# The layers' norm with tokens on partitions

## The reference

```
for i in range(DEPTH):                      # DEPTH = 6
    x = attn_layer(shift_tokens(x), Wqkv[i], q_scale[i], k_scale[i], Wo[i]) + x
    x = ffn_layer(shift_tokens(x), ln_g[i], ln_b[i], W1[i], b1[i], W2[i], b2[i]) + x

def ffn_layer(x, g, bln, W1, b1, W2, b2):
    mu = x.mean(-1, keepdims=True)
    var = ((x - mu) ** 2).mean(-1, keepdims=True)
    xn = (x - mu) / jnp.sqrt(var + 1e-05) * g + bln
    hg = xn @ W1 + b1
    a, gate = jnp.split(hg, 2, -1)
    return a * jax.nn.gelu(gate, approximate=False) @ W2 + b2
```

## Time and profile before

| | |
|---|---|
| median of 3 runs | 3917.49 us |
| profiled execution | 3918.71 us, its span 3916.9 us |
| TensorE busy | 3581.4 us, 91% of the span |
| VectorE busy | 3162.1 us, 81% |
| ScalarE busy | 2652.5 us, 68% |
| GpSimd busy | 2432.0 us, 62% |
| mean granted TensorE clock | 0.98 |
| chain that ended last | PE 53%, DVE 15%, issue 9%, ACT 7% |
| products by `meanw` in the layers, L1236 and L1242 | 52.7 and 49.1 us busy, 96 records each for 48 groups |
| VectorE's passes of the norm, L955, L975, L978 | 678, 746, 1242 ns each, 48 of each |
| ScalarE's, L698, L703, L705 | 631, 682, 630 ns each, 48 of each |

### The profile page before, as it was taken

How to read it: one execution, slowest core, us unless ns; L and a number is a source line. 1 busy time by engine, 2 the same in 40 slices (tenths; PEclk the granted TensorE clock), 3 DMA queues, 4 the chain that set the end, 5 groups by cost and what they waited for, 6 DMA issues and landing times.

```text
span 3916.9 us, 146395 instructions
## 1 busy us (share of the span) xinstructions
PE 3581.4 (91%) x60128; PEld 2226.2 (57%) x60128; DVE 3162.1 (81%) x4377; ACT 2652.5 (68%) x4972; POOL 2432.0 (62%) x2197
## 2 busy tenths in 40 slices
PE   5676776899999999999999999999999999999997
PEld 2222222566666666666666666666666666666664
DVE  4899998888878778888878788778787887888884
ACT  3555554677777777767776777677777777676765
POOL 0355554876666666666666666666666666666661
PEclk9889898999999999999999999999999999999999
DMA  3000000111111111111110111111111111110101
GB/s 76 0 0 0 0 0 0 34 32 31 31 42 41 34 30 31 31 47 38 35 32 26 42 42 36 32 31 31 45 37 33 31 31 47 36 36 27 32 28 37
DMA packets 64418, 120.05 MB, mean 31 GB/s; under 512 B 18196, under 2 KB 35986, under 8 KB 63634
## 3 DMA queue, kind: packets, MB, share of 16 engines
q1 hardware_dynamic: 63762, 110.70, 9.7%
HBM read 20.50 MB, written 2.10 MB: 6 GB/s over the span
## 4 chain that ended last, share of the span: by engine, by line
PE 53%; DVE 15%; issue 9%; ACT 7%; POOL 0%; ACTq 0%; DMA 0%; DVEq 0%; POOLq 0%; SPq 0%
PE ob L1187 10%; PE qk L1129 9%; PE sc L1214 7%; PE trb L1001 6%; PE vob L1195 4%; PE vob L1135 4%; PE sc L1163 4%; DVE arena L888 3%; PE sc L1221 3%; DVE ssq L894 3%; DVE mx L901 3%; PE ob L1001 2%; DVE arena L889 2%; ACT arena L619 2%; DVE xnT L978 1%
## 5 line engine op out<-in xcount | busy, mean ns | idle before, releaser
L507 POOL TENSOR_TENSOR arena<-arena,rnorm 128x512 f32<-128x512 f32 x768 | 793.7, 1054 | 929.3 <-ACT rnorm L626 928.8
L500 POOL TENSOR_TENSOR arena<-arena 128x512 f32<-128x512 f32 x768 | 961.7, 1274 | 84.9 <-DVE arena L889 84.9
L633 ACT ACTIVATE arena<-trb 128x512 f32<-128x512 f32 x768 | 465.7, 606 | 432.4 <-PE trb L1001 432.4
L1129 PE MATMUL qk<-wqkv,xs 128*128 128x512 f32 x1536 | 734.2, 601 | 16.0 <-issue 8.9
L888 DVE TENSOR_TENSOR arena<-qk,tab_q 128x512 f32<-128x512 f32 x384 | 263.7, 687 | 504.6 <-ACT arena L619 499.6
L483 POOL TENSOR_TENSOR arena<-arena 128x512 f32<-128x512 f32 x256 | 299.9, 1180 | 345.4 <-DVE arena L858 329.9
L1001 PE MATMUL trb<-ident,arena 128*128 128x128 f32 x3072 | 483.0, 280 | 10.7 <-ACT arena L633 7.6
L619 ACT ACTIVATE arena<-qk 128x512 f32<-128x512 f32 x768 | 433.5, 592 | 79.4 <-PE qk L1129 65.5
L1129 PEld LDWEIGHTS qk<-wqkv,xs 128*128 128x128 f32 x1536 | 294.5, 193 | 312.0 <-issue 294.8
L894 DVE TENSOR_REDUCE ssq<-arena 128x16 f32<-128x1024 f32 x384 | 464.3, 1209 | 0.0
L514 POOL TENSOR_TENSOR arena<-arena,rinv 128x512 f32<-128x512 f32 x384 | 392.4, 1043 | 65.8 <-DVE rinv L911 65.8
(11 more groups left out here) (139 smaller groups left out, 6020.5 us busy)
## 6 DMA issues: line engine op xcount, KB each, us to landing
arena<-arena SPq DMA_DIRECT2D x192, 384.0 KB, 3.2
arena<-arena SPq DMA_DIRECT2D x192, 64.0 KB, 3.0
wqkv<-in_L_ffn_Wqkv SPq DMA_DIRECT2D x18, 512.0 KB, 4.3
wo<-in_L_ffn_Wo SPq DMA_DIRECT2D x6, 512.0 KB, 4.0
arena<-in_L_attn_x SPq DMA_DIRECT2D x8, 256.0 KB, 2.8
out<-arena SPq DMA_DIRECT2D x8, 256.0 KB, 2.2
w<-in_L_ffn_W SPq DMA_DIRECT2D x6, 341.0 KB, 2.9
arena<-in_sel SPq DMA_DIRECT2D x1, 1024.0 KB, 5.0
```

The lines of the kernel that those rows point to most:

```text
L500: nc.gpsimd.tensor_tensor(ts[c * 2 + j][:, heads], tu[:, 0, heads], tu[:, 1, heads], ALU.add).then_inc(summed[0], 1)
L507: nc.gpsimd.tensor_tensor(part, part, rnorm[j][:, 8 * h:8 * h + 8].unsqueeze(2).to_broadcast([P, 8, HEAD]), ALU.mult) \
L633: A((qT, kT)[j][u][:, 4 * h:4 * h + 4, at_col:at_col + P], TRB.rearrange("p (a t) -> p a t", a=4), ACT.Copy) \
L1129: MM(QK[:, 512 * h:512 * h + 512], lhsT=xs[u][:, c * P:(c + 1) * P], rhs=wqkv[:, col:col + 512], start=True, stop=True) \
```

## The change

The centred tokens, their squares and their sums are made with tokens on partitions. Per group: in slot 3 four turns bring `xs2` into `VOB` (now behind the `up` products), and VectorE's `centre` sums each token's 128 features along the free axis and subtracts the mean (now behind `hidden`); in slot 4 ScalarE squares and VectorE sums the squares, at the end of its slot; in slot 5 ScalarE takes Ln and Exp of 128x4 numbers, VectorE multiplies (behind `rope`), four turns, behind the down products, bring the result back into the second half of `SC`, and ScalarE copies it out to `xnT` with weight and bias. The odd `v_unit` waits for `centre` to have read `VOB`; `scores` of slot 6 waits for the copy out. The layer's parameters are copied in slot 5.

```diff
-LAG_STAGE, LAG_MEAN, LAG_VAR, LAG_NORMED = 17, 19, 21, 22
+LAG_STAGE, LAG_TOKENS, LAG_SQUARES, LAG_BACK = 17, 19, 20, 21
...
@@ ScalarE, layer_slot
                 unit = unit_at(l, k, 0)
                 if unit:
                     squares(*unit)
+                at_ = group_at(l, k, LAG_BACK)
+                if at_:
+                    act_e.wait_ge(n_var[0], at_[1] + 1)
+                    A(nlog[:], nvar[:], ACT.Ln, scale=1.0 / DIM, bias=eps[:, 0:1]).then_inc(n_log[0], 1)
+                    act_e.wait_ge(n_log[0], at_[1] + 1)
+                    A(nrstd[:], nlog[:], ACT.Exp, scale=-0.5).then_inc(n_rstd[0], 1)
...
-                at_ = group_at(l, k, LAG_MEAN)
-                if at_:
-                    item(act_e, ln_xc, at_[1] + 2 * GROUPS)
-                    A(sq2[0], xc[0], ACT.Square).then_inc(ln_sq[0], 1)
-                at_ = group_at(l, k, LAG_VAR)
-                if at_:
-                    item(act_e, ln_var, at_[1] + 2 * GROUPS)
-                    item(act_e, ln_out, at_[1] + (2 * GROUPS - 1))
-                    A(rstd[0], bank[2][:], ACT.Ln, bias=eps[:, 0:1]).then_inc(ln_log[0], 1)
-                    item(act_e, ln_log, at_[1] + 2 * GROUPS)
-                    A(rstd[0], rstd[0], ACT.Exp, scale=-0.5).then_inc(ln_rstd[0], 1)
+                at_ = group_at(l, k, LAG_SQUARES)
+                if at_:
+                    act_e.wait_ge(n_xc[0], at_[1] + 1)
+                    A(sq2[0], xc[0], ACT.Square).then_inc(n_sq[0], 1)
+                at_ = group_at(l, k, LAG_BACK)
+                if at_:
+                    if at_[0] == 0:
+                        item(act_e, lpar_done, l + (k - LAG_BACK) // LAYER)
+                    item(act_e, n_back, at_[1])
+                    A(xnT[:, at_[0] * GROUP:at_[0] * GROUP + GROUP], SC[:, 512:1024], ACT.Identity, scale=lpar[:, 0:1], bias=lpar[:, 1:2]) \
+                        .then_inc(n_out[0], 1)
...
@@ VectorE
+            def centre(group, n):
+
+                dve.wait_ge(n_turned[0], n + 1)
+                tokens = VOB[:, :].rearrange("p (c f) -> p c f", f=DIM)
+                V.tensor_reduce(nsum[:], tokens, op=ALU.add, axis=AX.X).then_inc(n_sum[0], 1)
+                slot(dve, n_back, n)
+                dve.wait_ge(n_sum[0], n + 1)
+                V.scalar_tensor_tensor(out=xc[0].rearrange("p (c f) -> p c f", f=DIM),
+                                       in0=nsum[:, :].unsqueeze(2).to_broadcast([P, GROUP // P, DIM]), scalar=-1.0 / DIM,
+                                       in1=tokens, op0=ALU.mult, op1=ALU.add).then_inc(n_xc[0], 1)
...
                 if unit:
                     rope(*unit)
+                at_ = group_at(l, k, LAG_BACK)
+                if at_:
+                    dve.wait_ge(n_rstd[0], at_[1] + 1)
+                    tokens = xc[0].rearrange("p (c f) -> p c f", f=DIM)
+                    V.tensor_tensor(tokens, tokens, nrstd[:, :].unsqueeze(2).to_broadcast([P, GROUP // P, DIM]), ALU.mult).then_inc(n_scaled[0], 1)
                 at_ = step_at(l, k, LAG_SCORES)
                 if at_:
                     maxima(*at_)
-                at_ = group_at(l, k, LAG_MEAN)
-                if at_:
-                    item(dve, ln_mean, at_[1] + 2 * GROUPS)
-                    V.tensor_tensor(xc[0], xs2.rearrange("p s t -> p (s t)"), bank[2][:], ALU.subtract).then_inc(ln_xc[0], 1)
...
                     hidden(*at_, 1, 4, 0)
                     hidden(*at_, 2, 5, 512)
+                at_ = group_at(l, k, LAG_TOKENS)
+                if at_:
+                    centre(*at_)
                 at_ = group_at(l, k, LAG_DOWN)
                 if at_:
                     add_y(*at_)
...
                 if unit:
                     square_sums(*unit)
-                at_ = group_at(l, k, LAG_NORMED)
...
-                    V.scalar_tensor_tensor(out=xc[0], in0=xc[0], scalar=lpar[:, 0:1], in1=rstd[0], op0=ALU.mult, op1=ALU.mult) \
-                        .then_inc(ln_aff[0], 1)
-                    item(dve, ln_aff, at_[1])
-                    V.tensor_scalar(xnT[:, at_[0] * GROUP:at_[0] * GROUP + GROUP], xc[0], lpar[:, 1:2], None, ALU.add).then_inc(ln_out[0], 1)
+                at_ = group_at(l, k, LAG_SQUARES)
+                if at_:
+                    dve.wait_ge(n_sq[0], at_[1] + 1)
+                    V.tensor_reduce(nvar[:], sq2[0].rearrange("p (c f) -> p c f", f=DIM), op=ALU.add, axis=AX.X).then_inc(n_var[0], 1)
...
@@ TensorE, layer_slot
-                mean = group_at(l, k, LAG_MEAN)
-                if mean:
...
-                    MM(VOB[:, :], lhsT=meanw[:], rhs=xs2.rearrange("p s t -> p (s t)"), start=True, stop=True).then_inc(ln_mean[0], 1)
-                var = group_at(l, k, LAG_VAR)
-                if var:
...
-                    MM(VOB[:, :], lhsT=meanw[:], rhs=sq2[0], start=True, stop=True).then_inc(ln_var[0], 1)
+                tokens, back = group_at(l, k, LAG_TOKENS), group_at(l, k, LAG_BACK)
...
                         up(*at_, parts, scored)
+                if tokens:
+                    pe.wait_ge(ln_in[0], tokens[1] + 1)
+                    if out_before:
+                        item(pe, x_added, out_before[0])
+                    for c in range(GROUP // P):
+                        last = turn(VOB[:, c * P:(c + 1) * P], xs2.rearrange("p s t -> p (s t)")[:, c * P:(c + 1) * P], start=True, stop=True)
+                    last.then_inc(n_turned[0], 1)
...
                     down_product(*at_, scored)
+                if back:
+                    pe.wait_ge(n_scaled[0], back[1] + 1)
...
+                    for c in range(GROUP // P):
+                        last = turn(SC[:, 512 + c * P:512 + (c + 1) * P], xc[0][:, c * P:(c + 1) * P], start=True, stop=True)
+                    last.then_inc(n_back[0], 1)
...
                 if value and k % 2:
-                    if mean:
-                        item(pe, ln_xc, mean[1] + 2 * GROUPS)
-                    elif var:
-                        item(pe, ln_log, var[1] + 2 * GROUPS)
+                    if tokens:
+                        pe.wait_ge(n_xc[0], tokens[1] + 1)
                     elif out_before:
                         item(pe, x_added, out_before[0])
                     v_unit(value[0], value[1], value[2], value[5])
```

More of the change, by code:

```diff
@@ L154, in build @@
         rnorm = [sb(f"rnorm{u}", [P, HEADS]) for u in range(2)]
+        nsum = sb("nsum", [P, GROUP // P])
+        nvar = sb("nvar", [P, GROUP // P])
+        nlog = sb("nlog", [P, GROUP // P])
+        nrstd = sb("nrstd", [P, GROUP // P])
         mx = [sb(f"mx{n}", [P, 2 * STEP_HEADS]) for n in range(2)]
@@ L314, in build @@
         x_added = sem("x_added")
+        n_turned = sem("n_turned")
+        n_sum = sem("n_sum")
+        n_xc = sem("n_xc")
+        n_sq = sem("n_sq")
+        n_var = sem("n_var")
+        n_log = sem("n_log")
+        n_rstd = sem("n_rstd")
+        n_scaled = sem("n_scaled")
+        n_back = sem("n_back", 1)
+        n_out = sem("n_out")
         up_done = sem("up_done")
@@ L965, in layer_slot @@
                     add_y(*at_)
+                at_ = group_at(l, k, LAG_BACK)
+                if at_ and at_[0] == 0:
+                    layer = l + (k - LAG_BACK) // LAYER
+                    if group_at(l, k, LAG_DOWN):
+                        item(dve, x_next, layer * GROUPS + -1)
+                    V.tensor_copy(lpar[:], lpar_all[:, ds(layer, 1), :].rearrange("p o n -> p (o n)")).then_inc(lpar_done[0], 1)
+                    item(dve, lpar_done, layer)
                 if unit:
                     square_sums(*unit)
-                at_ = group_at(l, k, LAG_NORMED)
+                at_ = group_at(l, k, LAG_SQUARES)
                 if at_:
[L970 to L974, removed]
-                    V.scalar_tensor_tensor(out=xc[0], in0=xc[0], scalar=lpar[:, 0:1], in1=rstd[0], op0=ALU.mult, op1=ALU.mult) \
-                        .then_inc(ln_aff[0], 1)
-                    item(dve, ln_aff, at_[1])
-                    V.tensor_scalar(xnT[:, at_[0] * GROUP:at_[0] * GROUP + GROUP], xc[0], lpar[:, 1:2], None, ALU.add).then_inc(ln_out[0], 1)
+                    dve.wait_ge(n_sq[0], at_[1] + 1)
+                    V.tensor_reduce(nvar[:], sq2[0].rearrange("p (c f) -> p c f", f=DIM), op=ALU.add, axis=AX.X).then_inc(n_var[0], 1)
             dve.wait_ge(lpar_in[0], N_LPAR)
@@ L1141, in windows, with scores @@
                         yield b, g, g // 2 * P + b * SPAN + g % 2 * WINDOW
-            def scores(s, B, u, j, n, up0, up1, up2, down):
+            def scores(s, B, u, j, n, up0, up1, up2, down, back):
                 item(pe, tr_evac, B * (2 * UNITS) + (2 * UNITS - 2 + j))
@@ L1155, in scores @@
                     item(pe, x_next, down[1])
+                if back:
+                    pe.wait_ge(n_out[0], back[1] + 1)
                 for h in range(2):
@@ L1198, in up @@
             def up(group, n, parts, scored):
-                pe.wait_ge(ln_out[0], n + (1 + 2 * GROUPS + ln_out[1]))
```

(19 more changed lines are left out.)

9 lines of the change are left out of this document (1 added, 8 removed).

## The result

The changed kernel takes 4103.69 us, the median of four runs (4093.57 to 4106.04); the kernel before 3916.15 beside it (four runs). The ratio is 1.047, 95% interval 1.0447 to 1.0493. The forecast was 4078 us, the range 3975 to 4155: slower, as forecast, by 187 us instead of 161. The profiled execution took 4093.57 us, 175 more than that of before, with a granted clock of 0.952 in the mean (before 0.980).

A forecast was written before the change was run, and what follows sets the result against it. TensorE was taken to bound the layers. The profiled 3918.7 us plus 99 for stalls (2.16 per group, 46 groups) plus 61 for the clock minus 1.2 gave 4078 us, range 3975 to 4155.

The forecast's parts named there:

- The wait in slot 3: Slot 3: TensorE's odd value product waits 2.86 us for VectorE's centring; slot takes 10.78 us, +1.11 per group.
- The old wait: Slot 3: the mean product's wait for VectorE's add into xT, 57.7 us in 46 times, would be covered.
- slot 7: Slot 7: the up products lose their wait for the normed rows, -0.43 us per group.
- Slot 5: Slot 5: the turn back waits 1.24 us for VectorE's scaling, +0.93, plus +0.55 for GpSimd's interference, per group.
- the half clock: Slot 4, at 1.2 GHz: a late unit product delays ScalarE and VectorE alike, so the fall isn't made good.
- the collision with GpSimd: Slot 5: VectorE's scaling multiply meets GpSimd's two-input instructions, +0.55 us; ends 0 and 1.04.
- the lower end of my term: Slot 5: the scaling multiply finds a gap between GpSimd's instructions and loses 0 us.
- The upper end: Slot 5: a whole GpSimd instruction is ahead of the scaling multiply, costing 1.04 us.
- The clock: After slot 3's gap TensorE's clock halves in 3 of 4 groups, 1.78 us each: 1.34 per group, 61 us.
- gaps of 1.1 us amid the small products of `values`: Earlier trace: two gaps of some 1.1 us there were read as leaving TensorE's clock alone.
- the upper bound of the term: Slot 3: TensorE's clock falls behind the new gap in every group, 82 us.
- Rival 3: Slot 3's odd value product: VectorE isn't late, TensorE runs through; 119 us faster, 3799 us; chance 0.06.

The follow-up runs named there:

- b_norm21: The kernel before, with the norm's last two passes (weight, bias) at the end of VectorE's slot 5 instead of slot 6; 0.9925 of before.
- a_fill: The changed kernel with three useless 128x512 products in front of TensorE's wait for the centred tokens in slot 3; 1.0353 of before.
- a_centre: The changed kernel with VectorE's centring in front of the two hidden steps in slot 3 instead of behind them; 1.0381 of before.
- a_fs: The changed kernel with the scaling ahead of the rotation in slot 5 and three useless products before slot 3's wait; 1.0047 of before.
- c_tok2: The changed kernel with centring ahead of the rotation in slot 3, scaling right behind the add into xT in slot 5; 0.9832 of before.
- b_all: The kernel before with the mean product behind the up products, its subtraction before slot 3's rotation, the norm's last two passes in slot 5; 0.9819 of before.
- a_scale: The changed kernel with VectorE's scaling ahead of slot 5's rotation and ScalarE's small Ln and Exp ahead of its squares; 1.0206 of before.
- c_tok: The changed kernel with the scaling ahead of the rotation in slot 5 and the centring ahead of the rotation in slot 3; 0.9898 of before.

## Why the prediction was right

**The wait in slot 3** was the main term and came out as worked out. In the three periods in which the clock didn't fall in it the slot takes 10.75 us; the prediction said 10.78. The sum (0.68) and the subtraction (0.69, taken as 0.74) were priced from neighbours within 0.05.

**The old wait** is gone from slot 3 and the one of **slot 7** too (7.32 in the ordinary slots), as predicted; b_norm21 shows the latter alone.

**Slot 5** was put at +0.93 +0.55; its middle value is +0.73 (9.76), its mean +1.04 (two periods, in which the clock fell in slot 5, take 13.7 and 14.1). Two errors. The scaling started 4.38 us into the slot, not 4.70: I had said that the half clock delays VectorE and TensorE alike in slot 4, so that nothing is made good; in fact VectorE came out of it some 0.3 to 0.4 earlier relative to TensorE (the clamp L915 that ends slot 4's sums of squares is over at 2152.49, 0.40 before slot 5 starts; in the earlier trace rows it is over 0.01 after). Where the clock had not fallen, it started at 4.71, as worked out. And the collision with GpSimd cost 0.26 in the middle (0.94 instead of 0.68), not 0.55. It hangs on a few hundredths of a microsecond. In a_fill the multiply starts at 4.71, 0.03 ahead of GpSimd's next instruction, and takes 0.68: the lower end of my term, 0.

```profile
2145.97 0.68 DVE L983 TENSOR_TENSOR arena<-arena,nrstd 128x512 f32<-128x512 f32 x1
2146.00 3.02 POOL L513 TENSOR_TENSOR arena<-arena 128x512 f32<-128x512 f32 x2
```

The upper end, 1.04, was met too: with it the multiply takes 1.72, and it took 1.71 in a_centre, started 0.10 behind GpSimd's, and 1.60 to 1.81 in five groups of the changed kernel. The Trainium skill says (SBUF — State Buffer, "Who interferes with whom") that a VectorE instruction with two SBUF inputs and a GpSimd instruction that reads SBUF exclude each other, and that the order of issue decides who waits. These rows agree.

**The clock** was mis-sized. I took falls in 3 of 4 groups at 1.78 us, 1.34 per group. It fell in slot 3 in 41 of 44 and in slot 4 in one more, and a period with falls costs 0.9 in slot 3 and 1.1 in slot 4 over the clean values (11.65 and 9.16 in the middle, against 10.75 and 8.05). Slots 3 and 4 together are +3.02 us per group where my terms made 2.45: 26 us over 46 groups. Slot 5, 0.44 below its terms, took back 20 of them. With the 8 us outside the 46 periods the profiled execution is 14 us over the sum (175 against 161), and the other three took 8 to 12 us more than it, which makes the 26 by which the forecast is short of the median. That the fall itself costs, and not only the wait, is what a_fill and a_fs show.

One reading behind the 3 of 4 was wrong: that gaps of 1.1 us amid the small products of `values` left the clock alone. The trace of before has three of 1.12, each at the end of a layer, and behind two of them the clock fell (at 2229.20 and at 3297.71). Here is the first, with the window behind it:

```profile
2229.20 0.42 PE L1187 MATMUL ob<-arena 64*64 64x32 f32 x11 [1.12 <-issue]
...
2230.04 1.86 PE L1135 MATMUL vob<-wqkv,xs 128*128 128x512 f32 x2
2231.70 2.78 PE L1129 MATMUL qk<-wqkv,xs 128*128 128x512 f32 x4
```

```profile
2230.20:2233.40 3.20, 3.20 (x5) 1.13 (x4) 0.61 (x3) 2.47 (x5) 0.00 (x0) 0.50 0.02 5
```

These rows speak for a higher share of falls than 3 in 4 behind the longer gap of slot 3, toward the upper bound of the term.

What the prediction's sum has no term for are the gaps amid small products in slots 3 to 5: 23 in slot 3 of the changed kernel, of some 0.76 us. They cost nothing there, since TensorE then waits for `centre` anyway; in the faster kernels they are what is late next.

Rival 3, the gain from TensorE's shorter program, was real potential. Something like the 0.66 us is there in c_tok2: without gaps slot 3 takes 7.8 (b_all: 8.2), slot 5 8.61 (b_all: 9.03). But it decides where its condition said, at the place of `centre`, and needed three moves in the order to come within reach.

## What to carry to other kernels

Look up where a new step stands in its engine's written order, and what the bounding engine has queued behind it, before counting cycles: here the same instructions took 4.7% more or 1.7% less time than before by the order alone. Waits of one chain hang together: moving one step forward gives most of it back at the next meeting point until each is covered (a_centre alone gained 0.9%, on top of a_scale 2.6%), so test such edits together. And a wait of 2 to 3 us in TensorE's stream may cost another 2 us through the clock; here, filling it with useless products was faster than waiting (a_scale 1.0206, a_fs 1.0047).

## What the runs showed of the hardware

- A single gap of about 1 us let the clock fall to half when it lay amid the 64x32 products of `values`, with no other wait in the slot: 1.12 in the kernel before (two of three), 0.83, 1.11 and 1.23 in c_tok, 0.96 in c_tok2. In a_fill it fell behind 10 such gaps of 0.99 to 1.41, each some 3 us behind a wait of 1.0. Behind gaps of 1.26 us between full products it never did in 45 cases of the kernel before. But 22 of the 23 gaps in c_tok2's slot 3 left the clock alone too; what decides is open.
- TensorE's stream of small products (256 instructions in about 2 us) shows gaps of 0.4 to 1.5 us with no releaser: none in slots 3 to 5 of the kernel before, 23 in c_tok2's slot 3, 37 in a_fill's slot 5. In slot 3 they come at fixed slots of the layer's loop (in the changed kernel at slots 59, 3, 11, 19 and 27 of 64, not at 35, 43, 51), and the same in the five kernels that share TensorE's program with it; in a_fill and a_fs, whose program has three products more, slot 3 has one each. But the program isn't all: these two share it, and have 37 and 6 gaps in slot 5.
- These gaps end when instructions have just come in. The DMA records show packets of 16 KB of kind "instruction" on queue q8, one or two per slot. All 264 gaps of 0.4 us or more in slots 3 to 5, over the eleven profiles that have any (from slot 32 of the first layer on), end 1.2 to 1.6 us after such a packet has landed; of all moments in these slots only 5% lie so. That points to the supply of instructions. Why a packet comes late, no run tested.
- At the turn of the loop the changed kernel's gap was 3.9 us where it had been 2.2 (four times); in a_fill and a_fs it was 2.3 to 2.8. Why is open as well.
